# Head statistics from PSUM and a chain of three products for the gated sum of an attention tile

## What is computed

```python
out_cross = _ln(jnp.einsum('bts,bsc->btc', a, v), ln_cr_g, ln_cr_b)      # likewise out_dot, out_cos
fused = jnp.concatenate([out_cross, out_dot, out_cos], axis=-1)
gate = jax.nn.softmax(jnp.einsum('btc,gc->btg', fused, gw) + gb, axis=-1)
z = gate[..., 0:1] * out_cross + gate[..., 1:2] * out_dot + gate[..., 2:3] * out_cos
h = h + z
```

## Time and profile before

| what | us |
|---|---|
| median of 3 runs (range) | 1315.83 (1311.95 to 1317.48) |
| profiled execution | 1311.76 |
| its span, first to last instruction | 1309.8 |
| PE busy in the span | 1090.7 (83%) |
| DVE busy | 832.9 (64%) |
| POOL busy | 802.1 (61%) |
| ACT busy | 677.8 (52%) |

### The profile page before, as it was taken

The page is one execution under the profiler, slowest core; times in us unless marked ns, Lnnn a source line. Parts: engine busy times, 40 slices in busy tenths (PEclk is TensorE's granted clock), DMA queues, the critical chain, the costliest instruction groups (busy, mean ns, idle before and its releaser), DMA issues. The chain is left out here.

```text
span 1309.8 us, 23074 instructions
## 1 busy us (share of the span) xinstructions
PE 1090.7 (83%) x7468; PEld 961.3 (73%) x7468; DVE 832.9 (64%) x2539; ACT 677.8 (52%) x1703; POOL 802.1 (61%) x1252
## 2 busy tenths in 40 slices
PE   4789999998999999999999999999982248875762
PEld 3568888888898988888898888888871126664641
DVE  5456677777686767768686776877665874421110
ACT  1446755665665666666566666655653543421210
POOL 6276685776477667747766774555453006777784
PEclk9879999999999999999999999999995557898786
DMA  3010000010010101001010100000002002444442
GB/s 104 13 39 17 22 26 27 27 28 23 9 32 25 31 24 32 25 9 32 25 32 23 32 26 9 12 9 19 12 19 61 0 0 54 76 92 78 83 69 23
DMA packets 49082, 42.47 MB, mean 32 GB/s; under 512 B 6728, under 2 KB 44488, under 8 KB 48840
## 3 DMA queue, kind: packets, MB, share of 16 engines
q0 software_dynamic: 18432, 22.04, 8.8%
q1 hardware_dynamic: 30536, 19.00, 4.7%
HBM read 27.38 MB, written 13.63 MB: 31 GB/s over the span
## 5 line engine op out<-in xcount | busy, mean ns | idle before, releaser
L631 PE MATMUL mixed<-v,pT 128*128 128x132 f32 x2560 | 320.8, 277 | 1.4 <-DVE o L872 1.4
L631 PEld LDWEIGHTS mixed<-v,pT 128*128 128x128 f32 x2560 | 303.0, 190 | 3.0 <-issue 2.6
L866 DVE TENSOR_REDUCE neg_max<-scores 128x1 f32<-128x1024 f32 (+1 forms) x192 | 199.1, 1037 | 52.3 <-PE scores L434 51.7
L1095 POOL DMA_INDIRECT gram<-in_emb,ids x192 | 191.9, 1000 | 62.0 <-issue 52.6
L1023 ACT ACTIVATE probs<-scores,neg_max 128x1024 f32<-128x1024 f32 (+1 forms) x192 | 186.7, 973 | 59.6 <-DVE neg_max L866 59.5
L1032 ACT ACTIVATE pT<-turned 128x512 f32<-128x512 f32 x211 | 125.4, 595 | 64.8 <-PE turned L612 64.4
L1146 POOL TENSOR_TENSOR zb<-row,gate 128x384 f32<-128x384 f32 x64 | 54.7, 854 | 142.7 <-DVE gate L904 142.4
L612 PE MATMUL turned<-con,probs 128*128 128x128 f32 x844 | 124.8, 277 | 19.9 <-ACT probs L1023 8.1
L432 PE MATMUL scores<-k_hi,q_hi 128*128 128x512 f32 x320 | 135.5, 423 | 2.3 <-DVE q_lo L768 2.3
L434 PE MATMUL scores<-k_hi,q_lo 128*128 128x512 f32 x320 | 126.4, 395 | 0.0
L433 PE MATMUL scores<-k_lo,q_hi 128*128 128x512 f32 x320 | 125.8, 393 | 0.0
(11 more groups left out here) (304 smaller groups left out, 2431.7 us busy)
## 6 DMA issues: line engine op xcount, KB each, us to landing
wd<-in_w_down SPq DMA_DIRECT2D x32, 171.0 KB
token_table<-w SPq DMA_DIRECT2D x16, 320.0 KB, 2.4
out_h<-h SPq DMA_DIRECT2D x16, 256.0 KB, 2.3
gram<-in_emb,ids POOLq DMA_INDIRECT x192, 2.6
wu<-in_w_up SPq DMA_DIRECT2D x8, 170.5 KB, 3.8
w<-in_weights SPq DMA_DIRECT2D x1, 1174.0 KB, 7.8
xg<-token_table,slots POOLq DMA_INDIRECT x64, 2.7
out_h<-yw,slots POOLq DMA_INDIRECT x64, 3.4
```

The source lines that it names most:

```text
L631: last = pe.matmul(mixed[:, 0:VW], pT[:, n % 2, j * P:(j + 1) * P], vals, start=(j == 0), stop=(last_half and j == half * 4 + 3))
L866: dve.tensor_reduce(neg_max[:, n % 4:n % 4 + 1], scores[:, (n % 2) * S:(n % 2) * S + width], AX_X, ALU.max, negate=True).then_inc(maxed, 1)
L1095: pool.indirect_dma_start(gram[:, t % 4, g, :], None, emb[g], bass.IndirectOffsetOnAxis(ap=ids[:, s, t, g:g + 1], axis=0)).then_inc(gather ...
```

## The change

Of each unit, `output` now does two instructions on PSUM: `bn_stats` on `mixed[:, 0:128]` (signals `o_stats`), and a product of `mixed` with a new tile `gain` (the rows `ln_g`, and 1.0 for the logit columns) that writes `o` and signals `o_ok`. `tile_stats` keeps only the `bn_aggr`. The three products of `tile_gate` become a chain: the first adds `h`, each later one adds the result before it, and waits for it by the new semaphore `u_part`. POOL multiplies `ln_b` by the gate as before, folds the three into one, and adds `u` once, 128 wide. At the start two instructions fill `gain`.

```diff
@@ setup on DVE
+                dve.memset(gain[:, :, C:VW], 1.0)
+                dve.tensor_copy(gain[:, :, 0:C], R("ln_g").rearrange("p (i c) -> p i c", c=C))
@@ output(n), DVE
-                dve.tensor_copy(o[:, t % 4, br, :], mixed[:, 0:VW]).then_inc(o_ok, 1)
+                dve.bn_stats(st[:, t % 2, br, :], mixed[:, 0:C]).then_inc(o_stats, 1)
+                dve.tensor_tensor(o[:, t % 4, br, :], mixed[:, 0:VW], gain[:, br, :], ALU.mult).then_inc(o_ok, 1)
@@ tile_stats(n), DVE
-                dve.wait_ge(o_ok, BR * n + BR)
-                for br in range(BR):
-                    last = dve.bn_stats(st[:, m, br, :], o[:, n % 4, br, 0:C])
-                last.then_inc(o_stats, 1)
-                dve.wait_ge(o_stats, n + 1)
+                dve.wait_ge(o_stats, BR * n + BR)
@@ tile_gate(n), DVE
                 for br in range(BR):
-                    last = dve.scalar_tensor_tensor(out=u[:, m, br, :], in0=o[:, n % 4, br, 0:C],
-                                                    scalar=gate_r[:, m, br:br + 1], in1=R("ln_g")[:, br * C:(br + 1) * C],
-                                                    op0=ALU.mult, op1=ALU.mult)
-                last.then_inc(u_ok, 1)
+                    if br:
+                        dve.wait_ge(u_part, n * (BR - 1) + br)
+                    last = dve.scalar_tensor_tensor(out=u[:, m, br, :], in0=o[:, n % 4, br, 0:C], scalar=gate_r[:, m, br:br + 1],
+                                                    in1=u[:, m, br - 1, :] if br else h[:, (b % 2) * NT + t, :],
+                                                    op0=ALU.mult, op1=ALU.add)
+                    last.then_inc(u_part if br < BR - 1 else u_ok, 1)
@@ tile_sum(n), POOL
-                pool.wait_ge(z_g, n * 4 + 1)
-                pool.tensor_tensor(zb[:, m, 0, :], zb[:, m, 0, :], h[:, (b % 2) * NT + t, :], ALU.add).then_inc(z_g, 1)
-                pool.wait_ge(z_g, n * 4 + 2)
+                for br in range(1, BR):
+                    pool.wait_ge(z_g, n * BR + br)
+                    pool.tensor_tensor(zb[:, m, 0, :], zb[:, m, 0, :], zb[:, m, br, :], ALU.add).then_inc(z_g, 1)
+                pool.wait_ge(z_g, n * BR + BR)
                 pool.wait_ge(u_ok, n + 1)
-                pool.tensor_tensor(u[:, m, :, :], u[:, m, :, :], zb[:, m, :, :], ALU.add).then_inc(z_g, 1)
-                pool.wait_ge(z_g, n * 4 + 3)
-                pool.tensor_tensor(u[:, m, 0, :], u[:, m, 0, :], u[:, m, 1, :], ALU.add).then_inc(z_g, 1)
-                pool.wait_ge(z_g, n * 4 + 4)
...
-                pool.tensor_tensor(h1[:, t, :], u[:, m, 0, :], u[:, m, 2, :], ALU.add).then_inc(h1_ok, 1)
+                pool.tensor_tensor(h1[:, t, :], u[:, m, BR - 1, :], zb[:, m, 0, :], ALU.add).then_inc(h1_ok, 1)
```

More of the change, by code:

```diff
@@ L214, in build_program @@
         bias_row = asb("bias_row", [P, 3 * VW])
+        gain = asb("gain", [P, BR, VW])
         inv_temp = asb("inv_temp", [P, 1])
@@ L340, in build_program @@
         scale_ok = sem("scale_ok")
+        u_part = sem("u_part")
         u_ok = sem("u_ok")
@@ L907, in tile_gate @@
                     dve.wait_ge(h1_ok, n - 1)
+                t, b = n % NT, n // NT
                 for br in range(BR):
-                    last = dve.scalar_tensor_tensor(out=u[:, m, br, :], in0=o[:, n % 4, br, 0:C],
-                                                    scalar=gate_r[:, m, br:br + 1], in1=R("ln_g")[:, br * C:(br + 1) * C],
-                                                    op0=ALU.mult, op1=ALU.mult)
-                last.then_inc(u_ok, 1)
+                    if br:
[4 more added lines that the diff above has]
+                    last.then_inc(u_part if br < BR - 1 else u_ok, 1)
             def tile_h1_stats(n):
```

## The result

| | before | after |
|---|---|---|
| median of 4 runs, us (range) | 1313.89 (1310.89 to 1317.48) | 1275.69 (1274.70 to 1276.83) |
| ratio, 95% interval | | 0.9714 (0.9700 to 0.9729) |
| profiled execution; its span | 1311.76; 1309.8 | 1274.70; 1272.9 |
| POOL busy | 802.1 | 734.6 |
| DVE busy | 832.9 | 823.9 |

The kernel is 38.2 us faster. The direction and the two places that the prediction named were right; the size was not. Run twice more beside a fresh set of the kernel before, the change gave 36.3 and 38.1 us.

The account below looks back on a forecast made before the run. PE was taken to bound the loop, waiting on DVE's late branch-2 slot and POOL's backlog. Waits of 18.2 us times 0.7, less 1 us for `o_ok`, plus 2.5 us tail: 14.2 us faster, 1301.6 us, range 1293 to 1312 us.

Parts of the forecast that it names:

- The sum of the waits: PE's idle waits in the loop: exponentials, evictions, `pT` and first sequence together save 18.2 us before any discount.
- rival B: Only the branch-2 slot works, POOL's saving falls into its idle time: 8.5 us faster, 1307.3 us; chance 0.18.
- After: 0.20 + 0.285 + about 0.10 = 0.58 us: DVE's branch-2 slot, output's start to first `bn_aggr`: 1.09 us before, 0.58 us after, so maxima come 0.5 us sooner.
- The chain takes 0.14 us of it back: DVE's chained products ahead of the branch-2 slot: 0.14 us more a tile, leaving 0.36 to 0.5 us, 0.43 taken.
- I keep 0.7 of it: Discount on the loop's 18.2 us, since other producers stay late: 12.7 us kept, bounds 0.3 and 1.0.
- POOL: the mechanism: POOL's shorter sum brings `h1` 1.3 to 1.6 us sooner, removing 6.4 us of `pT` waits and DVE's `h1` wait.
- The statistics' own cost: DVE reading PSUM: 0.28 us for the new `bn_stats`, 0.285 us for the new product.
- The branches 0 and 1, 1 us: In these slots the output takes 0.20 us more; DVE has room, and the later `o_ok` for `mix` costs 1 us.
- The tail, 2.5 us: Chain behind the last `mix` up to the experts: earlier statistics and shorter POOL sums save 2.5 us.
- A: The forecast itself: DVE's late slot and POOL's backlog both reach PE; 1301.6 us, 1295 to 1308; chance 0.54.
- C: PE's waits only change names, so only the tail's gain remains, less 1 us: 1314.3 us; chance 0.19.
- D: Slower: chained DVE products and POOL's operations block each other, branch-2 maxima come 0.4 us later: 1325 us; chance 0.09.

## Why the prediction was off, point by point

**What bounds the kernel: right.** PE bounds the loop, DVE's branch-2 slot and POOL's queue reach it. The runs with one half each show both, and the moved statistics show that the place in the slot decides.

**The sum of the waits, the step that failed.** The loop was to gain 18.2 us before the factor, and 11.7 us after it and the 1 us for `o_ok`; it gained 35.5 us. The factor of 0.7 took only 5.5 us of this. At a factor of one the whole forecast would have been 19.7 us, half of the 38.2 us. It is the terms under the factor that were too small (us of PE's idle time in the loop):

| term | forecast | fell, before to after |
|---|---|---|
| exponentials | 3.9 + 3.4 = 7.3 | 15.2 to 2.5: 12.7 |
| `pT` | 6.4 | 10.5 to 1.4: 9.1 |
| evictions `q_lo` and `v` of the loop | 3.5 | 9.0 to 4.0: 5.0 |
| PE's busy time | 0 | some 6 |

Three things made them small. A wait for exponentials was charged with the 0.43 us of its own slot; eighteen such waits fell by 0.7 us each on average. The waits for `pT` were counted from 200 to 880 us alone and under two names; over the whole loop and under all four they were 10.5 us. And the part of the wait that shows as busy time was not in the sum at all. Split by part, the statistics had 10.0 us before the factor (the figure of rival B) and took 19.3 us out of the loop; POOL's part had 8.2 us and took 12.5 us out of it. In the last sequence alone 3.4 us were charged and 6.5 us came: the maxima there cannot account for all of it by the mean delay, which fell by 0.59 us, 4.7 us in eight tiles. Why a wait that is taken away brings more than its slot is shorter, and why part of it shows as busy, stays open.

**"After: 0.20 + 0.285 + about 0.10 = 0.58 us", 0.5 us sooner: too small.** Measured 0.62 against 1.33 us from output to maxima, 0.71 us. The new `bn_aggr` was charged both the product's full 0.285 us and a wait on its own result. They overlap: it starts 0.20 us behind the product. Less what the products grew by, that is 0.56 us, near the 0.59 us by which the mean delay fell; 0.43 us had been taken.

**The chain takes 0.14 us of it back: the sum right by luck.** The mean did grow by 0.15 us (1.53 to 1.68 us), as forecast, but not by the chain alone: with POOL's part and no chain it is 1.64 us already, and the change without the chain has 1.61 us, so the chain's own share is some 0.05 to 0.07 us. The time without it is the same within 0.5 us.

**"I keep 0.7 of it": a discount that the last sequence does not bear out.** The reason given was that something else would be late next. In the last sequence PE had only the eight waits for exponentials and 1.2 us of others, and the table above shows that nothing is lost there. In the first seven sequences something is: the statistics alone give 12.8 us for 37 us of delay. But there too the forecast, which counted only nine waits, came out below what was measured.

**POOL: the mechanism right, its size half.** Forecast were 6.4 us of `pT` and half of the 3.5 us of evictions, times 0.7, and 2.2 us of the tail: 7.9 us. Measured with POOL's part alone, 14.7 us. Of the 10.5 us of waits for `pT` this part alone leaves 5.5 us, and together with the statistics 1.4 us. DVE's waits for POOL fell as forecast, if not to nothing. The wait for `h1`, is now 1.5 us at its longest:

```profile
612.06 0.29 DVE L921 BATCH_NORM_STATS2 st<-h 128x6 f32<-128x128 f32 x1 [1.47 <-POOL h L1159]
```

How the 14.7 us divide among `pT`, evictions and the rest of POOL's queue, the runs don't say.

**The statistics' own cost: right.** 292 ns for the `bn_stats` from PSUM (0.28 taken), 275 ns for the product (0.285 taken). The same read from SBUF took 282 ns, so PSUM costs 10 ns here. The 65 ns more per instruction that the prediction estimated from the Trainium skill, page "VectorE: DVE Perf Modes", errata section, are not seen, and DVE is 9.0 us less busy, where that estimate made it 12.4 us more for the new reads.

**The branches 0 and 1, 1 us: of the right order.** 1 to 4 us by the two runs with one more `bn_stats`.

**The tail, 2.5 us: nearly right**, 1.7 us.

**The rivals.** A's bounds add up to 1296 to 1309 us and not to 1295 to 1308 us; the measured time lies outside either. C, waits under other names, happened only with one half alone: for `o`, 1.4 to 4.7 us, with the statistics; for `q_lo`, 3.6 to 6.5 us, with POOL's part, where `v` gave 2.0 us of it back. B falls by POOL's 14.7 us. D falls: products of 1.72 us as before in the disturbed tiles, and the chain is free. The lock itself is there: the version with a shorter `zb` is 6.5 us faster. The Trainium skill, page "SBUF — State Buffer", section "Who interferes with whom", says that such DVE and GpSimd instructions exclude each other for a whole instruction, and the trace agrees: the two products stood until POOL's instructions ended, 1.34 us beside a `zb` of 0.86 us and 1.12 us beside one of 0.65 us; with one fold behind `zb` they end 0.15 us behind that fold in both (561.75 and 561.90, 560.02 and 560.17). The prediction used this rule against the change, and not to ask what a shorter POOL instruction would bring.

**Not settled:** why one batch ran everything 1 to 2% slower. There the first scores came at about 70 us instead of 65 us, and the first sequence was 5 to 8 us longer than in the repeats; the granted clock over the span is the same (0.92). Ratios from it are given, and no cause rests on them.

## What to carry to other kernels

Where one engine's in-order queue feeds a chain over several engines, ask what stands between the ready input and the instruction that the chain waits for: moving three short statistics out of that place was worth 22.6 us of 1314 us, and moving them two instructions back 19.1 us, on an engine that is busy 64% of the time. If the trace shows the same wait once in each tile and next to nothing else, as in the last sequence, count such a gain in full; where other work stands between, as in the first seven, measure it. Count what is waited for over the whole loop and under every name, and take the idle time of the engine that waits as the lower end. Where two engines' instructions hold each other up, the length of the one that runs beside the path may matter more than the other engine's total work; one version here points to it.

## What was unexpected

- An independent instruction between a producer and its reader seems to hide the wait on an own result: `bn_aggr` started 0.20 us behind the start of the product, where before it stood 0.10 us behind the end of its `bn_stats`.
- The chain by semaphores costs three undisturbed products 0.24 us (0.87 us in the earlier trace rows, 507.41 to 508.52 after, below), and the kernel nothing that can be measured.

```profile
507.41 0.34 DVE L913 SCALAR_TENSOR_TENSOR u<-o,gate_r,h 128x128 f32<-128x128 f32 x1
...
507.78 0.74 DVE L913 SCALAR_TENSOR_TENSOR u<-o,gate_r,u 128x128 f32<-128x128 f32 x2
```

- With a shorter POOL instruction beside DVE's products, 256 wide for 384, these were 0.22 us a tile shorter and the kernel 6.5 us, while a whole POOL instruction of 0.46 us less brought nothing.
